# W up and W down in ten pieces with a count for each step, contexts a batch earlier: a fused attention and FP4 feed-forward kernel

## The chip, the cores and the metric

The kernel runs on one NeuronCore of a Trainium2 chip. The metric is the device time of one execution in microseconds (us), from the program's start to its end. The profile gives a span, from the first instruction to the last, which is 1.8 us shorter than the time of the same execution.

## The reference

What is computed, for 16 batches of 256 rows by 256 columns:

```python
# x, ctx: (16, 256, 256); w_gate, w_up: (704, 256); w_down: (256, 704); all float32
q, k, v = heads(layernorm(x)), heads(ctx), heads(ctx)     # 16 heads of 16 columns
x = x + softmax(q @ k.T / 4) @ v                          # for each head
z = layernorm(x)
h = silu(fp4(z) @ fp4(w_gate).T) * (fp4(z) @ fp4(w_up).T)
out = x + fp4(h) @ fp4(w_down).T
# fp4(a): blocks of 16 along the last axis; scale = max(|block|) / 6;
#         each element goes to the nearest of 0, .5, 1, 1.5, 2, 3, 4, 6, times sign and scale
```

## The kernel before, in words

The kernel has two stages: attention over 16 batches (up to about 245 us of the span), then the feed-forward net over 32 tiles of 128 rows (from about 285 us). The change touches the first alone. Each engine has its own hand-written program, and semaphores tie them.

**Attention.** One step of TensorE computes the 16 heads of a batch t: the scores (SC), which ScalarE turns into exponentials (P), and the products with the values (PV). Heads stand as (g, j), four groups of four. In the same step TensorE also computes a second product of queries and keys (MX), 22 heads ahead, for which VectorE finds each row's maximum (`maximum`, MF<-MX). MX has two banks, so that the product of one head waits until the reduction of the head two before it is done (`max_scores`). The maxima of a batch are split into two bfloat16 parts (MP), turned by TensorE, copied by ScalarE (MT), and put by a small DMA (QS<-MT) as two more rows below that batch's queries. The first scores of a batch wait for that DMA (`scores`, semaphore m_stacked).

**SyncE's queue.** Nearly every DMA is issued by SyncE, in order (`attention_step` of SyncE). Its step t waits for the last part of the keys of batch t+3 (k_low) and issues six copies KS<-KP of 128 KB; waits for the maxima of batch t+1 and issues QS<-MT; waits for the third part of the queries of batch t+3 (q_out), which ScalarE writes at the very end of its step t, and issues six copies QS<-QP; then it loads from HBM, 256 KB each, the two layouts QN and KT of batch t+5, the context C of batch t+2, and x (X) of batch t. Since it waits for the end of ScalarE's step t, the second half of SyncE's step t is issued while TensorE is already in step t+1.

**Weights.** The three weight matrices lie in one tile W of 4608 columns, cut into 16 slices of 288. In step t VectorE reduces slice t+1 to its block maxima (`weight_maxima`, wmax<-W), after the reduction of head (1, 1), and later finds scales; GpSimd and ScalarE scale and round; each slice goes through in one step and part of the next. W gate fills the first third of the slices, W up the second, W down the last. W gate is loaded in the first steps; W up and W down are loaded by `load_weights` at the ends of SyncE's steps 0 to 3. VectorE waits for W gate in step 0 and for W up in step 4 (`st.first == RING`), and for W down at the end of step 4.

**Values.** GpSimd copies the context C into the layout of the values (VA<-C), for batch t+1 in step t.

The steps of SyncE from -1 to 14 are made by `steps(sp, attention_step, -1, RING, 1, RING, B - 1, B)`: steps -1 to 3 written out, 4 to 7 in a loop of one turn, the rest written out. The other engines loop over four steps, three times.

Of the kernel before, what the change touches and what calls it, by code (L numbers as in the profile page):

```python
# [12 lines left out]
B, S, D = 16, 256, 256  # L13
H, DK = 16, 16
QT = S // 128
FI = 704
# [18 lines left out]
RING = 4  # L35
IDENTS, CONSTS = 4, 9
AHEAD = 22
LEAD = 3
# [34 lines left out]
def steps(eng, body, begin, start, turns, period, end, count):  # L73


    for t in range(begin, start):
        body(Step(t, count, period))
    with eng.Fori(0, turns) as i:
        for c in range(period):
            body(Step(start + c, count, period, i))  # L80
    for t in range(start + turns * period, end):
        body(Step(t, count, period))
# [6 lines left out]
def ffn_steps(eng, body):  # L89
    steps(eng, body, 0, 5, (TILES - 10) // 2, 2, TILES + 3, TILES)  # L90


def program(nc, x, x_p, ctx_in, ctx_t, wg_in, wu_in, wd_in, out):
# [8 lines left out]
    with es:  # L102
# [6 lines left out]
        def sem(name):  # L109
            return es.enter_context(nc.semaphore(name))  # L110
# [3 lines left out]
        WN = [W[:, m * NT * D:(m + 1) * NT * D].rearrange("p (r c) -> p r c", c=D) for m in range(2)]  # L114
        WD = W[:, 2 * NT * D:].rearrange("p (r c) -> p r c", r=2)
# [96 lines left out]
        sc_ready, exp_done = sem("sc_ready"), sem("exp_done")  # L212
        pv_done, pv_out = sem("pv_done"), sem("pv_out")
        o_den, o_norm, x1_ready = sem("o_den"), sem("o_norm"), sem("x1_ready")
        w_zeroed, w_begun, w_loaded = sem("w_zeroed"), sem("w_begun"), [sem(f"w_loaded{m}") for m in range(3)]
        w_seq, w_scaled, w_abs, w_c, w_grid, w_done = (sem(n) for n in
            ("w_seq", "w_scaled", "w_abs", "w_c", "w_grid", "w_done"))
        ones_ready, ones_last = sem("ones_ready"), sem("ones_last")
# [18 lines left out]
        def tiles(b):  # L237

            return bass.ds(b * (QT * D), QT * D)

        def gate(eng):

            eng.sem_inc(passed, 1)
# [38 lines left out]
        @block.sync  # L282
        def _(sp):
            def load_first(b, r):
                sp.dma_start(QN[r][:, :, :, :, :].rearrange("p q e d a -> p q (e d a)"),
                             xp_d[:, bass.ds(b * QT, QT), :]).then_inc(qn_loaded[r], 16)
                sp.dma_start(KT[r][:, :], t_d[:, bass.ds(b, 1), :].rearrange("p a c -> p (a c)")).then_inc(kt_loaded[r], 16)

            def load_context(b, r):
                sp.dma_start(C[r][:, :, :], c_d[:, bass.ds(b * QT, QT), :]).then_inc(c_loaded[r], 16)  # L290

            def load_x(b, r):
                sp.dma_start(X1[:, tiles(b)].rearrange("p (q c) -> p q c", q=QT),
                             x_d[:, bass.ds(b * QT, QT), :]).then_inc(x_loaded[r], 16)

            def stack(dst, parts, order, r):


                for j, p in enumerate(order):
                    sp.dma_start(dst[j:PROD:6, :, :].rearrange("d h t -> d (h t)"),  # L300
                                 parts[:, p, :]).then_inc(stacked[r], 16)

            def load_blocks(m, w, lo, hi, done):
                sp.dma_start(WN[m][:, lo:hi, :], w[lo * 128:hi * 128, :].rearrange("(r p) c -> p r c", p=128)
                             ).then_inc(done, 16)

            def load_last(m, w):
                full = FI // 128
                sp.dma_start(WN[m][0:FI - full * 128, full, :], w[full * 128:FI, :]).then_inc(w_loaded[m], 16)

            def load_down(r):
                sp.dma_start(WD[:, r, 0:FI], wd_in[128 * r:128 * (r + 1), :]).then_inc(w_loaded[2], 16)

            def load_weights(t):

                if t == -1:
                    load_blocks(0, wg_in, 2, 5, w_loaded[0])
                    load_last(0, wg_in)
                if t == 0:
                    load_blocks(1, wu_in, 0, 3, w_loaded[1])  # L320
                if t == 1:
                    load_blocks(1, wu_in, 3, 5, w_loaded[1])
                    load_last(1, wu_in)
                if t in (2, 3):
                    load_down(t - 2)

            def part(dst, parts, p, rows, r):
                for j in rows:
                    sp.dma_start(dst[j:PROD:6, :, :].rearrange("d h t -> d (h t)"), parts[:, p, :]).then_inc(stacked[r], 16)

            def first_keys(b):

                for n, rows in enumerate(((0, 3, 5), (1, 4))):
                    sp.wait_ge(k_out, 2 * b + n + 1)
                    part(KS[b], KP[b], n, rows, b)
                sp.wait_ge(k_low, b + 1)
                part(KS[b], KP[b], 2, (2,), b)

            def first_queries(b):
                for n, rows in enumerate(((0, 1, 2), (3, 4), (5,))):  # L340
                    sp.wait_ge(q_out, 3 * b + n + 1)
                    part(QS[b], QP[b], n, rows, b)

            load_first(0, 0)
            load_first(1, 1)
            load_first(2, 2)
            first_keys(0)
            first_queries(0)
            first_keys(1)
            first_queries(1)  # L350
            load_context(0, 0)
            sp.wait_ge(w_zeroed, 4)
            load_blocks(0, wg_in, 0, 2, w_begun)
            load_first(3, 3)

            def attention_step(st):
                if st.has(LEAD):
                    r = st.slot(LEAD, RING)
                    sp.wait_ge(k_low, st.times(LEAD, 1, 1))
                    gate(sp)  # L360
                    sp.wait_ge(sc_ready, st.times(0, H, 1))
                    gate(sp)
                    stack(KS[r], KP[st.slot(LEAD, 2)], (0, 1, 2, 0, 1, 0), r)
                if st.has(1):
                    sp.wait_ge(mt_ready, st.times(1, 1, 1))
                    gate(sp)
                    r = st.slot(1, 2)
                    sp.dma_start(QS[st.slot(1, RING)][PROD:ROWS, :, :].rearrange("d h t -> d (h t)"),
                                 MT[r][:, :]).then_inc(m_stacked[r], 16)
                if st.first == -1:  # L370
                    load_context(1, 1)
                    load_weights(-1)
                if st.has(LEAD):
                    sp.wait_ge(q_out, st.times(LEAD, 3, 3))
                    gate(sp)
                    stack(QS[r_q(st)], QP[st.slot(LEAD, 2)], (0, 0, 0, 1, 1, 2), r_q(st))
                if st.has(LOADS):
                    load_first(st.item(LOADS), st.slot(LOADS, RING))
                if st.first >= 0 and st.has(2):
                    load_context(st.item(2), st.slot(2, RING))  # L380
                if st.has(0):
                    load_x(st.item(0), st.slot(0, RING))
                if st.first >= 0:
                    load_weights(st.first)

            def r_q(st):
                return st.slot(LEAD, RING)

            def ffn_step(st):
                if st.has(-3):  # L390
                    r = st.slot(-3, 2)
                    sp.wait_ge(out_ready, st.times(-3, 1, 1))
                    gate(sp)
                    sp.dma_start(o_d[:, bass.ds(st.item(-3), 1), :].rearrange("p a c -> p (a c)"),
                                 OB[r][:, :]).then_inc(stored[r], 16)

            steps(sp, attention_step, -1, RING, 1, RING, B - 1, B)
            attention_step(Step(B - 1, B, RING))
            attention_step(Step(B, B, RING))
            ffn_steps(sp, ffn_step)  # L400
            for r in range(2):
                sp.wait_ge(stored[r], 16 * (TILES // 2))
# [369 lines left out]
        def _(dve):  # L772
# [64 lines left out]
            def weight_maxima(st):  # L837

                if st.first == -SCALE:
                    dve.wait_ge(w_begun, 16)  # L840
                elif st.first == 0:
                    dve.wait_ge(w_loaded[0], 32)
                elif st.first == RING:
                    dve.wait_ge(w_loaded[1], 48)
                dve.wait_ge(w_scaled, st.times(SCALE, 1))
                nc.vector.tensor_reduce(wmax[:, :], blocks(wslice(st, SCALE)), AX.X, ALU.max,
                                        apply_absolute_value=True).then_inc(w_seq, 1)
# [30 lines left out]
            def attention_step(st):  # L878
# [3 lines left out]
                for g in range(NG):  # L882
                    for j in range(HG):
# [18 lines left out]
                            weight_inverses(st)  # L902
                        if (g, j) == (2, 3) and st.has(GRID):
                            round_weights(st)
                        if (g, j) == (3, 3) and st.first == RING:
                            dve.wait_ge(w_loaded[2], 32)
                        if st.first == B - 1 and HG * g + j < LOTS:
                            weights_out(HG * g + j)

# [424 lines left out]
```

## Time and profile before

| | |
|---|---|
| median of 3 runs | 531.11 us (529.82 to 535.19) |
| profiled execution | 529.71 us, span 527.9 us |
| busy in the span | TensorE 486.9 us (92%), VectorE 435.1 (82%), ScalarE 373.8 (71%), GpSimd 302.3 (57%) |
| granted clock | 1.0 all through attention, 0.7 to 0.9 for some 50 us around the change of stages |
| DMA | 48.97 MB, nearly all of it before 245 us, at some 180 to 220 GB/s |
| W up | one load of 384 KB, one of 256 KB, one of 64 KB |
| W down | two loads of 352 KB |

PE is TensorE, PEld its weight loads, DVE VectorE, ACT ScalarE, POOL GpSimd and SP SyncE. A q behind an engine's name is its sequencer: SyncE's DMA issues are shown as SPq, and their duration is the time for which the queue is held, not that of the transfer. L846 is line 846 of the kernel. In a timeline a row can hold several instructions (x6), its second column then reaches from the first one's start to the last one's end, and in brackets stands how long the engine was idle and what ended that.

### The profile page before, as it was taken

What the parts mean: (1) busy time and instruction counts of PE and PEld (TensorE: products, weight loads), DVE (VectorE), ACT (ScalarE), POOL (GpSimd) and SP (SyncE); (2) the same over time, 40 slices, a digit from 0 to 9 for tenths busy, and PEclk for the clock granted to TensorE, in tenths of its full rate; (3) what the DMA queues carried; (4) which work ended last, traced back from release to release, by engine and by line L of the source; (5) the groups of instructions that cost most, each with busy time, mean ns of one, the idle gap of its engine ahead of it and who ended that gap; (6) DMA issues with size and microseconds to landing.
All of it is one profiled execution on the core that took longest, in us unless ns stands there. A gap on an engine that the chain in (4) does not pass through costs nothing.

```text
span 527.9 us, 13628 instructions
## 1 busy us (share of the span) xinstructions
PE 486.9 (92%) x4036; PEld 383.1 (73%) x4036; DVE 435.1 (82%) x1129; ACT 373.8 (71%) x740; POOL 302.3 (57%) x423
## 2 busy tenths in 40 slices
PE   1889899999999999997857899999999999999996
PEld 0245565666666666654437899999999999999996
DVE  3788899899999999886345888898889998889764
ACT  5569899999999999977653565556656566665653
POOL 7754465556566665443144566666676666766542
PEclk9999999999999999999877899999999999999999
DMA  7784878766666666521000000000000000000000
GB/s 215 215 220 126 212 197 220 226 192 178 191 185 182 176 186 179 149 88 43 0 2 0 2 21 20 10 20 20 20 20 10 20 20 20 20 10 21 23 21 30
DMA packets 49985, 48.97 MB, mean 93 GB/s; under 512 B 4768, under 2 KB 47648, under 8 KB 49952
## 3 DMA queue, kind: packets, MB, share of 16 engines
q1 hardware_dynamic: 49952, 48.58, 32.8%
q8 instruction: 15, 0.25, 0.2%
q14 instruction: 18, 0.15, 0.1%
HBM read 18.94 MB, written 4.19 MB: 44 GB/s over the span
## 4 chain that ended last, share of the span: by engine, by line
PE 73%; DVE 7%; issue 5%; POOL 4%; SPq 4%; ACT 4%; DMA 3%; POOLq 0%; DVEq 0%; ACTq 0%
PE SC L1182 22%; PE PV L1182 12%; PE PV L1130 9%; PE MX L1112 9%; PE SC L1098 7%; DVE MF L783 4%; PE T L1207 4%; SPq L300 3%; DMA QS<-MT 2%; PE T L1212 2%; PE T L1077 2%; PE T L1045 2%; PE SC L1207 1%; PE T L1052 1%; ACT P L611 1%
## 5 line engine op out<-in xcount | busy, mean ns | idle before, releaser
L783 DVE TENSOR_REDUCE MF<-MX 128x2 f32<-128x512 f32 x256 | 164.2, 685 | 19.0 <-PE MX L1112 16.2
L611 ACT ACTIVATE P<-SC 128x512 f32<-128x512 f32 x256 | 140.3, 594 | 19.8 <-PE SC L1098 17.8
L1112 PE MATMUL MX<-KS,QS 96*128 96x256 bf16 x512 | 102.9, 284 | 4.3 <-DVE MF L783 2.5
L1098 PE MATMUL SC<-QS,KS 98*128 98x256 bf16 x512 | 98.5, 274 | 3.6 <-DMA QS<-MT 3.5
L534 POOL TENSOR_TENSOR HQ<-HN,hscale 128x704 f32<-128x704 f32 x31 | 43.1, 1391 | 61.3 <-DVE HN L936 61.3
L716 ACT ACTIVATE HH<-T 128x768 fp32r<-128x768 f32 x31 | 25.2, 813 | 67.9 <-PE T L1207 67.9
L1130 PE MATMUL PV<-P,VA 128*32 128x256 f32 x1024 | 70.0, 392 | 0.9 <-ACT OT L620 0.9
L1098 PEld LDWEIGHTS SC<-QS,KS 98*128 98x128 bf16 x512 | 43.4, 97 | 35.7 <-ACT P L611 20.0
L1182 PE MATMUL SC<-WH,XH 128*128 128x352 f32 x256 | 68.7, 350 | 0.0
L1112 PEld LDWEIGHTS MX<-KS,QS 96*128 96x128 bf16 x512 | 43.9, 99 | 31.6 <-DVE MF L783 23.3
L1182 PE MATMUL SC<-WH,XL 128*128 128x352 f32 x256 | 62.9, 327 | 0.0
L1182 PE MATMUL SC<-WL,XH 128*128 128x352 f32 x256 | 62.9, 327 | 0.0
L1130 PEld LDWEIGHTS PV<-P,VA 128*32 128x32 f32 x1024 | 27.3, 110 | 25.6 <-ACT P L611 7.1
L1182 PEld LDWEIGHTS SC<-WL,XH 128*128 128x128 f32 x256 | 45.6, 192 | 0.0
L1182 PEld LDWEIGHTS SC<-WH,XL 128*128 128x128 f32 x256 | 45.3, 191 | 0.1
L521 POOL TENSOR_TENSOR HN<-HN,hinv 128x704 f32<-128x704 f32 x31 | 43.1, 1390 | 1.0 <-DVE hinv L1026 0.9
L916 DVE TENSOR_TENSOR HN<-SC,SG 128x352 f32<-128x352 f32 x64 | 33.3, 521 | 11.3 <-PE SC L1182 10.1
L1182 PEld LDWEIGHTS SC<-WH,XH 128*128 128x128 f32 x256 | 41.4, 194 | 1.6
L685 ACT ACTIVATE SG<-SC 128x352 f32<-128x352 f32 x64 | 29.4, 460 | 18.0 <-PE SC L1182 13.4
L529 POOL TENSOR_TENSOR frstd<-fve,mhalf 128x2 f32<-128x2 f32 x32 | 22.1, 691 | 22.5 <-DVE fve L983 22.5
L486 POOL TENSOR_TENSOR W<-W,WC 128x288 f32<-128x288 f32 (+1 forms) x16 | 12.7, 796 | 38.8 <-DVE WC L857 38.8
L576 ACT ACTIVATE QP<-T 128x512 bf16<-128x512 f32 x48 | 28.6, 595 | 6.5 <-PE T L1052 3.6
(138 smaller groups left out, 1029.8 us busy)
## 6 DMA issues: line engine op xcount, KB each, us to landing
KS<-KP SPq DMA_DIRECT2D x96, 128.0 KB, 3.1
QS<-QP SPq DMA_DIRECT2D x96, 128.0 KB, 2.4
QN<-in_x_p SPq DMA_DIRECT2D x16, 256.0 KB, 3.1
KT<-in_ctx_t SPq DMA_DIRECT2D x16, 256.0 KB, 3.1
C<-in_ctx SPq DMA_DIRECT2D x16, 256.0 KB, 4.2
X<-in_x SPq DMA_DIRECT2D x16, 256.0 KB, 4.9
out<-OB SPq DMA_DIRECT2D x32, 128.0 KB, 1.7
W<-in_L_ffn_w_down SPq DMA_DIRECT2D x2, 352.0 KB, 6.0
```

The lines of the kernel that those rows point to most:

```text
L521: nc.gpsimd.tensor_tensor(blocks(HN[r][:, :]), blocks(HN[r][:, :]), each(hinv[r][:, :]), ALU.mult).then_inc(hm_ready, 1)
L534: nc.gpsimd.tensor_tensor(blocks(HQ[r][:, 0:FI]), blocks(HN[r][:, :]), each(hscale[r][:, :]), ALU.mult).then_inc(hq_ready, 1)
L576: nc.scalar.activation(parts[:, n, :], bank, ACT.Copy).then_inc(out_sem, 1)
L611: nc.scalar.activation(P[g % 2][:, j, :, :], SC[h % 3][:, :, :], ACT.Exp, scale=0.25).then_inc(exp_done, 1)
L685: nc.scalar.activation(SG[a][:, :], G, ACT.Silu).then_inc(silu_done, 1)
L783: nc.vector.tensor_reduce(MF[st.slot(off, 2)][:, :, h:h + 1], MX[h % 2][:, :, :], AX.X, ALU.max, negate=True).then_inc(mx_done, 1)
L916: nc.vector.tensor_tensor(HN[st.slot(0, 2)][:, a * FH:(a + 1) * FH], U, SG[a][:, :], ALU.mult).then_inc(h_done, 1)
L1098: last = nc.tensor.matmul(SC[h % 3][:, k, :], KS[r][0:ROWS, h, k * 128:(k + 1) * 128], QS[r][0:ROWS, h, :], start=True, stop=True)
L1112: last = nc.tensor.matmul(MX[h % 2][:, q, :], QS[r][0:PROD, h, q * 128:(q + 1) * 128], KS[r][0:PROD, h, :], start=True, stop=True)
L1130: last = nc.tensor.matmul(PV[32 * j:32 * (j + 1), g % 2, :], VA[r][:, k, HG * g + j, :], P[g % 2][:, j, k, :], start=(k == 0), stop=(k == ...
L1182: mm = nc.tensor.matmul(dst, x[:, c, :], w[:, c, :], start=(first and i == 0), stop=(last and i == len(chunks) - 1))
L1207: return nc.tensor.matmul(dst, src, ident[:, :], start=first, stop=False, is_transpose=True, skip_group_check=True)
```

## The change

W up and W down are loaded in ten pieces: the five blocks of 128 rows of W up (128 KB each) in SyncE's steps 1 to 5, its last 64 rows (64 KB) in step 6, and each half of W down in two parts of 384 and 320 columns (192 and 160 KB) in steps 7, 8, 10 and 11. A piece stands behind the load of X, the last DMA of its step. Step t signals on one of three semaphores in turn (w_piece). At the end of each step t from 0 to 14, SyncE waits for the piece of step t-1, if there is one, and adds one to w_ready. VectorE waits for the count t ahead of `weight_maxima` in each step t from 1 on, in place of its waits for W up and W down in step 4.

The context is loaded three batches ahead in place of two, ahead of QN and KT in place of behind them. SyncE's steps are all written out.

```diff
-        w_zeroed, w_begun, w_loaded = sem("w_zeroed"), sem("w_begun"), [sem(f"w_loaded{m}") for m in range(3)]
+        w_zeroed, w_begun, w_loaded, w_ready = sem("w_zeroed"), sem("w_begun"), sem("w_loaded"), sem("w_ready")
+        w_piece = [sem(f"w_piece{r}") for r in range(3)]
...
-            def load_last(m, w):
+            def load_last(m, w, done):
                 full = FI // 128
-                sp.dma_start(WN[m][0:FI - full * 128, full, :], w[full * 128:FI, :]).then_inc(w_loaded[m], 16)
-
-            def load_down(r):
-                sp.dma_start(WD[:, r, 0:FI], wd_in[128 * r:128 * (r + 1), :]).then_inc(w_loaded[2], 16)
-
-            def load_weights(t):
-
-                if t == -1:
-                    load_blocks(0, wg_in, 2, 5, w_loaded[0])
-                    load_last(0, wg_in)
-                if t == 0:
-                    load_blocks(1, wu_in, 0, 3, w_loaded[1])
-                if t == 1:
-                    load_blocks(1, wu_in, 3, 5, w_loaded[1])
-                    load_last(1, wu_in)
-                if t in (2, 3):
-                    load_down(t - 2)
+                sp.dma_start(WN[m][0:FI - full * 128, full, :], w[full * 128:FI, :]).then_inc(done, 16)
+
+            def load_down(r, lo, hi, done):
+                sp.dma_start(WD[:, r, lo:hi], wd_in[128 * r:128 * (r + 1), lo:hi]).then_inc(done, 16)
+
+            PIECES = {t + 1: t for t in range(FI // 128 + 1)}
+            DOWN = {7: (0, 0, 384), 8: (0, 384, FI), 10: (1, 0, 384), 11: (1, 384, FI)}
+
+            def load_piece(t):
+
+                done = w_piece[t % 3]
+                if t in DOWN:
+                    load_down(*DOWN[t], done)
+                elif t in PIECES and PIECES[t] < FI // 128:
+                    load_blocks(1, wu_in, PIECES[t], PIECES[t] + 1, done)
+                elif t in PIECES:
+                    load_last(1, wu_in, done)
+
+            def piece_landed(t):
+
+                turns = sum(1 for u in (*PIECES, *DOWN) if u <= t - 2 and u % 3 == (t - 2) % 3)
+                if turns:
+                    sp.wait_ge(w_piece[(t - 2) % 3], 16 * turns)
+                sp.sem_inc(w_ready, 1)
...
                 if st.first == -1:
                     load_context(1, 1)
-                    load_weights(-1)
+                    load_blocks(0, wg_in, 2, 5, w_loaded)
+                    load_last(0, wg_in, w_loaded)
...
+                if st.has(LEAD):
+                    load_context(st.item(LEAD), st.slot(LEAD, RING))
                 if st.has(LOADS):
                     load_first(st.item(LOADS), st.slot(LOADS, RING))
-                if st.first >= 0 and st.has(2):
-                    load_context(st.item(2), st.slot(2, RING))
                 if st.has(0):
                     load_x(st.item(0), st.slot(0, RING))
-                if st.first >= 0:
-                    load_weights(st.first)
+                load_piece(st.first)
+                if 1 <= st.first + 1 < B:
+                    piece_landed(st.first + 1)
...
-            steps(sp, attention_step, -1, RING, 1, RING, B - 1, B)
-            attention_step(Step(B - 1, B, RING))
-            attention_step(Step(B, B, RING))
+            for t in range(-1, B + 1):
+                attention_step(Step(t, B, RING))
...
                 if st.first == -SCALE:
                     dve.wait_ge(w_begun, 16)
                 elif st.first == 0:
-                    dve.wait_ge(w_loaded[0], 32)
-                elif st.first == RING:
-                    dve.wait_ge(w_loaded[1], 48)
+                    dve.wait_ge(w_loaded, 32)
+                else:
+                    dve.wait_ge(w_ready, st.times(0, 1))
...
-                        if (g, j) == (3, 3) and st.first == RING:
-                            dve.wait_ge(w_loaded[2], 32)
```

SyncE, its step 1 from the copies of the queries on and the first copies of step 2; before:

```order
L300 DMA QS<-QP 16x8x512 [waits q_out]
L300 DMA QS<-QP 16x8x512 x5
L285 DMA QN<-in_x_p 128x2x256
L287 DMA KT<-in_ctx_t 128x512
L290 DMA C<-in_ctx 128x2x256
L293 DMA X<-in_x 128x2x256
L304 DMA W<-in_L_ffn_w_up 128x2x256
L309 DMA W<-in_L_ffn_w_up 64x256
L300 DMA KS<-KP 16x8x512 [waits k_low,sc_ready]
```

The same place in the changed kernel, here step 2, which has the first wait for a piece behind it:

```order
L301 DMA QS<-QP 16x8x512 [waits q_out]
L301 DMA QS<-QP 16x8x512 x5
L291 DMA C<-in_ctx 128x2x256
L286 DMA QN<-in_x_p 128x2x256
L288 DMA KT<-in_ctx_t 128x512
L294 DMA X<-in_x 128x2x256
L305 DMA W<-in_L_ffn_w_up 128x256
L301 DMA KS<-KP 16x8x512 [waits w_piece1,k_low,sc_ready]
```

The load of W is one block, C stands first, and ahead of the next keys stands the wait for the piece of the step before, followed by the addition to w_ready, which has no row.

VectorE, inside its loop, around the block maxima of a slice; before:

```order
L782 REGISTER_ALU
L783 TENSOR_REDUCE MF<-MX 128x2 [waits mx_ready]
L845 ISA
L846 ISA [waits w_scaled]
L846 TENSOR_REDUCE wmax<-W 128x18
L782 REGISTER_ALU
L783 TENSOR_REDUCE MF<-MX 128x2 [waits mx_ready]
```

And in the changed kernel:

```order
L791 REGISTER_ALU
L792 TENSOR_REDUCE MF<-MX 128x2 [waits mx_ready]
L853 ISA
L854 REGISTER_ALU [waits w_ready]
L855 ISA [waits w_scaled]
L855 TENSOR_REDUCE wmax<-W 128x18
L791 REGISTER_ALU
L792 TENSOR_REDUCE MF<-MX 128x2 [waits mx_ready]
```

A wait for w_ready now stands between the reductions of heads (1, 1) and (1, 2), in every turn of the loop and in steps 13 and 14 behind it. No other engine's instructions are moved.

## Rows read from the trace of the kernel before

**Rows 1.** Cores: span and mean granted TensorE clock

```profile
core 0: 527.9 us, clock 0.981
```

**Rows 2.** Stretches: us, busy of PE, PEld, DVE, ACT, POOL; clock, DMA share, GB/s

```profile
62.00:76.00 14.00, 12.73 (x128) 8.35 (x128) 11.73 (x30) 11.98 (x25) 7.12 (x12) 1.00 0.81 210
90.00:104.00 14.00, 12.93 (x137) 7.74 (x135) 12.24 (x30) 12.26 (x26) 7.71 (x12) 1.00 0.71 207
...
132.00:146.00 14.00, 13.87 (x146) 8.82 (x145) 13.12 (x32) 13.26 (x29) 8.34 (x13) 1.00 0.68 193
...
244.00:258.00 14.00, 10.28 (x93) 6.20 (x92) 5.88 (x20) 9.21 (x21) 6.00 (x11) 0.88 0.15 40
```

**Rows 3.** Waits: who waited for whom, us in total, times, longest

```profile
POOL VA L471 <- DMA C<-in_ctx: 30.4, 12, 5.6
...
PE SC L1098 <- DMA QS<-MT: 3.5, 5, 1.5
```

**Rows 4.** Timeline of PE at the starts of batches 1 and 2 (start, us)

```profile
47.34 0.28 PE L1098 MATMUL SC<-QS,KS 98*128 98x256 bf16 x1 [0.66 <-DMA QS<-MT]
...
60.57 1.07 PE L1130 MATMUL PV<-P,VA 128*32 128x256 f32 x16
63.14 0.39 PE L1098 MATMUL SC<-QS,KS 98*128 98x256 bf16 x2 [1.50 <-DMA QS<-MT]
```

**Rows 5.** Chain of waits ahead of batch 2 (start, us)

```profile
58.79 4.23 DMA QS<-MT
```

**Rows 6.** DMA issues of W up: KB each, us to landing

```profile
W<-in_L_ffn_w_up SPq DMA_DIRECT2D x1, 384.0 KB, 7.6
```

**Rows 7.** Timeline of ACT: last query part of step 5

```profile
120.51 0.59 ACT L576 ACTIVATE QP<-T 128x512 bf16<-128x512 f32 x1
```

**Rows 8.** Timeline of SyncE's queue, ends of steps 0, 1, 5, 11 and 12

```profile
52.32 0.47 SPq L287 DMA_DIRECT2D KT<-in_ctx_t  x1
53.23 0.37 SPq L290 DMA_DIRECT2D C<-in_ctx  x1
53.65 0.46 SPq L293 DMA_DIRECT2D X<-in_x  x1
54.16 0.46 SPq L304 DMA_DIRECT2D W<-in_L_ffn_w_up  x1
...
68.05 0.47 SPq L293 DMA_DIRECT2D X<-in_x  x1
...
121.19 3.80 SPq L300 DMA_DIRECT2D QS<-QP  x6
125.03 0.60 SPq L285 DMA_DIRECT2D QN<-in_x_p  x1
...
126.70 0.47 SPq L293 DMA_DIRECT2D X<-in_x  x1
...
209.89 0.51 SPq L293 DMA_DIRECT2D X<-in_x  x1
...
224.16 0.49 SPq L293 DMA_DIRECT2D X<-in_x  x1
```

**Rows 9.** Timeline of DVE around wmax in steps 1, 2, 6, 12 and 13

```profile
52.75 0.44 DVE L846 TENSOR_REDUCE wmax<-W 128x18 f32 x1
...
68.56 0.44 DVE L846 TENSOR_REDUCE wmax<-W 128x18 f32 x1
...
126.37 0.44 DVE L846 TENSOR_REDUCE wmax<-W 128x18 f32 x1
...
126.92 1.29 DVE L783 TENSOR_REDUCE MF<-MX 128x2 f32<-128x512 f32 x2
...
210.58 0.44 DVE L846 TENSOR_REDUCE wmax<-W 128x18 f32 x1
...
224.41 0.44 DVE L846 TENSOR_REDUCE wmax<-W 128x18 f32<-128x288 f32 x1
```

**Rows 10.** Timeline of PE: max-product of head (2, 1), step 6

```profile
128.27 0.39 PE L1112 MATMUL MX<-KS,QS 96*128 96x256 bf16 x2
```

## The prediction

> **What bounds it now.** I read the span and clock first [rows 1], then the busy time by stretch [rows 2], then who waits for whom [rows 3], and last the queues of one attention step side by side [rows 4 to 10]. The profiled execution takes 529.7 us against a median of 531.1 us of the three runs shown, so it lies 1.4 us under the median; the sum below is made against the 529.7. In an undisturbed stretch of attention TensorE is busy 13.87 of 14.00 us and VectorE 13.12 [rows 2], and one batch takes 14.03 us. So TensorE sets the pace and VectorE has under one microsecond to spare. The three stretches 62:76, 90:104 and 244:258 show TensorE under that: the first two hold waits for the small transfer of the maxima (QS<-MT), of which there are five with 3.5 us together and 1.5 us at most [rows 3]. 0.66 us of it lies before batch 1 and 1.50 us before batch 2 [rows 4]; the other three, before batches 3, 4 and 5, share 3.5 - 0.66 - 1.50 = 1.3 us. That of batch 2 is seen in the chain of waits: the transfer takes 4.23 us [rows 5], behind the 384 KB of W up issued at 54.16, which took 7.6 us to land [rows 6, 8].
>
> **How one step runs.** I call the start of batch t's scores on TensorE the start of step t. Take t = 6. ScalarE ends the last query part of the step before at 120.51 + 0.59 = 121.10 [rows 7]. Only then can SyncE issue the six QS<-QP copies, and behind them the loads: the last one, X, ends its issue at 126.70 + 0.47 = 127.17 [rows 8]. All this belongs to SyncE's step 5, so SyncE is well into the time of step 6 when its step 5 ends. VectorE reads the slice's maxima (wmax) of step 6 at 126.37 [rows 9], which is 0.80 us before that.
>
> **The change part by part.**
>
> *A new wait on VectorE.* SyncE now adds one to w_ready at the end of each step 0 to 14, and VectorE waits ahead of wmax in step t for the count t, thus for the end of SyncE's step t-1. Before, only steps -1, 0 and 4 waited for weights. This is the term that decides. For t = 6: SyncE is through X 0.80 us after VectorE wants to go on; the piece of W issued behind X costs what the W load cost, 0.51 us from one start to the next (53.65 to 54.16) [rows 8]; and wait, count, and VectorE's two waits take time that no row has by itself. Its bounds are 0.06 us (a max-product follows the reduction that frees its bank by about that, 128.21 to 128.27) [rows 9, 10] and 0.4 us (the gap between KT's end and C's start at 52.79 to 53.23, a SyncE gap with nothing to issue) [rows 8]; nothing of it can be below zero, since it stands between two things in order. I take 0.20, nearer the lower end, as four short sequencer steps. So VectorE stands still 0.80 + 0.51 + 0.20 = 1.51 us.
>
> Does that reach TensorE? Queued behind wmax on VectorE are the reductions of the next heads. They start 0.55 us after wmax and take 1.29 us for two, thus end at 128.21 [rows 9]; the max-product that needs the second one's bank starts at 128.27 [rows 10], 0.06 us later, as tight as two engines get. So there is no slack, and TensorE, which runs in order, loses all of the wait. Nothing gives it back: TensorE has 0.13 us idle in a step.
>
> The same for the other steps. Eight steps (3 to 9 and 11) are like t = 6: 8 x 1.51 = 12.08 us. Step 1: X ends at 53.65 + 0.46 = 54.11, wmax at 52.75 [rows 8, 9], no piece yet: 1.36 + 0.20 = 1.56. Step 2: X ends at 68.52, wmax at 68.56 [rows 8, 9], but wmax stands there 1.50 us late because of the wait before batch 2, which goes (below): 1.46 + 0.51 + 0.20 = 2.17. Step 10 has no piece ahead: 1.00. Step 12, where the layouts are loaded no more: X ends 210.40, wmax 210.58, with a piece: -0.18 + 0.71 = 0.53. Step 13, without: 224.65 against 224.41, 0.24 + 0.20 = 0.44 [rows 8, 9]. Step 14 waits for nothing. Sum 12.08 + 1.56 + 2.17 + 1.00 + 0.53 + 0.44 = 17.8 us more.
>
> *The big W loads gone from steps 0 to 3.* No W stands ahead of the KS<-KP copies of step 1, and 128 KB instead of 320 to 352 in the next three. The transfer of the maxima is ready as late as TensorE lets it, while the KS<-KP copies ahead of it hang on statistics made before wmax. With VectorE's stall in between, the queue has 1.5 us more to drain. So all four waits from batch 2 on go: 3.5 - 0.66 = 2.9 us less. That of batch 1 stays. What is late next is VectorE, priced above.
>
> *Pieces in steps 1 to 8, 10 and 11.* Ten issues in place of five (two up, one last rows, two down). Their data, at most 192 KB, goes beside the step, with a whole step until it is asked for. Their issues lie on the path, since VectorE waits for the count behind them; they are in the 17.8. Cost as transfers: nothing, covered by the 1.5 us just named. If that cover were gone, the maxima's transfer would be late by up to 1.5 us as before batch 2.
>
> *Contexts a batch earlier and ahead of the layouts.* GpSimd waits 30.4 us in 12 waits for them [rows 3]. It hides: TensorE and VectorE show no wait on it (VA is wanted a batch later). The same four loads in another order end at the same time; the extra context goes to step -1, when SyncE afterwards waits for GpSimd anyway. Zero. *The loop of SyncE written out* had one turn of four steps: the same instructions, zero.
>
> Sum: 17.8 - 2.9 = 14.9 us, thus 529.7 + 14.9 = 544.6 us.
>
> *A rule against pieces.* SyncE's issue of W took 0.46 us [rows 8] and it went on at once, so a piece costs the queue 0.51 us. The Trainium skill (DMA: Bandwidth & Descriptors, section Rules for kernel authors) says to coalesce many small transfers, and its section on the anatomy of one DMA gives some 2.0 us fixed for each on the GpSimd path. Were the queue held so long for each of ten pieces, the page's estimate would be 10 x 1.5 = 15 us more, near 560 us. The same section lays most of it to completion, not to the issue, and by that the trace agrees.
>
> **Rivals.**
>
> (a) *The count comes in time, or VectorE's stall is hidden.* Then only the 2.9 us count: 526.8 us, no slower than before. The mechanism is the empty queue; it decides if SyncE ends its step 1.5 us sooner against VectorE than I read, at 126.37 instead of 127.88. For it: nothing in the rows of steps 3 to 11; steps 12 and 13 come near. Against it: six copies of 3.80 us cannot start before ScalarE's 121.10. That the change does not do what it says, with the wait satisfied early, is this case too. Chance 0.07.
>
> (b) *Part of the stall is absorbed.* VectorE has 14.00 - 13.12 = 0.88 us idle in a step. If half of it lay behind wmax, 13 x 0.44 = 5.7 us come back: 538.9 us. Against it, 128.21 and 128.27. Chance 0.12.
>
> (c) *TensorE's clock falls in the new pauses.* Between 244 and 258 us TensorE was busy 10.28 of 14 us and granted 0.88 of the clock [rows 2], a mix of 2.4 and 1.2 GHz: 12% of 14 us is 1.7 us. In thirteen steps that is 22 us: 567 us. Against it: busy 12.73 and 12.93 of 14 us, with the 1.5 us pause among them, kept 1.00 [rows 2], and 13.87 of 15.5 is the like of it. By the Trainium skill (TensorE: Matmul & The Clock Gate, section HAM oscillation) a waiting pause in every round can throttle the array each round; no run here shows it in attention. Chance 0.05.
>
> My forecast has 0.76.
>
> **Numbers.** The likeliest time is 544.6; measured beside a median like the one shown it would read some 0.5 us more, 545. The forecast alone, with 0.06 and 0.4 for the signal (13 x -0.14 and 13 x +0.2) and 1.4 us for the median, runs from 542 to 549. The range takes in (b) below and a little above: 538 to 550. About 1% (5.3 us) is what a measurement of this kernel can tell from no change. Forecast, (b) and (c) are slower by over 1%; of (a) most is within 1% (526.8 is 0.6% less). Faster 0.02, same 0.06, slower 0.92.
>
> **What would show it.** VectorE idle before each wmax of steps 1 to 13 by 1.0 to 2.2 us, in steps 12 and 13 by half of one; the batches of steps 3 to 9 15.5 us apart instead of 14.03; max-products waiting for MF in (2,0) and (2,1); no wait of TensorE for QS<-MT but that of batch 1; GpSimd's 30 us wait for contexts gone, with nothing gained by it; clock 1.00 until 250 us. I am wrong if wmax has no idle time ahead of it, or if it has and the batches stay 14 us apart.

## The result

| | before | changed |
|---|---|---|
| median of the runs of one session | 531.85 us (529.82 to 535.19, 4 runs) | 543.33 us (542.41 to 545.56, 4 runs) |
| ratio | | 1.0216 (95% interval 1.0153 to 1.0278) |
| profiled execution, its span | 529.71, 527.9 us | 543.28, 541.5 us |
| a second session | 531.68 us (19 runs) | 543.70 us (4 runs), ratio 1.0208 (1.0160 to 1.0256) |

The change makes the kernel 2% slower. Forecast were 545 us (538 to 550), and 544.6 against the profiled execution, which measured 543.3.

### The profile page after: what moved, and what is told of

The parts are those of the page before. It is cut to its first block, busy times and chain, and to the rows that moved or that the text cites. A ratio compares the mean times of both kernels' runs of the same rounds, so it can differ in the third digit from the quotient of the medians.

```text
span 541.5 us, 13656 instructions
## 1 busy us (share of the span) xinstructions
PE 493.0 (91%) x4036; PEld 384.1 (71%) x4036; DVE 434.1 (80%) x1129; ACT 375.2 (69%) x740; POOL 301.9 (56%) x423
## 4 chain that ended last, share of the span: by engine, by line
PE 60%; SPq 13%; issue 8%; ACT 7%; DVE 6%; POOL 3%; DMA 1%; DVEq 0%; ACTq 0%; POOLq 0%
PE SC L1189 21%; PE PV L1189 12%; SPq L301 7%; PE MX L1119 6%; PE PV L1137 5%; PE SC L1105 4%; ACT P L620 4%; PE T L1214 4%; DVE MF L792 3%; PE T L1219 2%; PE T L1052 2%; ACT QP L585 1%; PE SC L1214 1%; SPq L291 1%; SPq L286 1%
## 5 line engine op out<-in xcount | busy, mean ns | idle before, releaser
L792 DVE TENSOR_REDUCE MF<-MX 128x2 f32<-128x512 f32 x256 | 163.1, 685 | 16.0 <-PE MX L1119 14.9
L1105 PE MATMUL SC<-QS,KS 98*128 98x256 bf16 x512 | 99.9, 278 | 0.7 <-DMA QS<-MT 0.7
```

The lines of the kernel that those rows point to most:

```text
L792: nc.vector.tensor_reduce(MF[st.slot(off, 2)][:, :, h:h + 1], MX[h % 2][:, :, :], AX.X, ALU.max, negate=True).then_inc(mx_done, 1)
L1105: last = nc.tensor.matmul(SC[h % 3][:, k, :], KS[r][0:ROWS, h, k * 128:(k + 1) * 128], QS[r][0:ROWS, h, :], start=True, stop=True)
```

## The profile after

The list of waits of the changed kernel (engine, line, waited for: us in total, times, longest) has a new row high up, with the sequencer of SyncE as the releaser:

```profile
POOL W L495 <- DVE WC L866: 86.7, 16, 10.9
...
DVE wmax L855 <- SPq L333: 17.7, 13, 2.2
...
PE MX L1119 <- DVE MF L792: 14.1, 19, 1.8
```

VectorE waits 17.7 us in 13 steps for the count; the forecast had 17.8 us in 13. TensorE in its turn waits for VectorE's reductions. GpSimd's wait for contexts [rows 3] is not in the list any more, but GpSimd has won nothing: it now stands longer in its next wait, for WC. The waits for the maxima's transfer, 3.5 us of TensorE in [rows 3], are nearly gone. The page's costliest groups show it in the scores' row (last columns: busy, mean ns; idle before, releaser):

```profile
L1105 PE MATMUL SC<-QS,KS 98*128 98x256 bf16 x512 | 99.9, 278 | 0.7 <-DMA QS<-MT 0.7
```

One step in full, the same batch 6 as in [rows 7 to 10], which now starts at 127.22. First ScalarE's last query part, then SyncE's queue:

```profile
126.77 0.59 ACT L585 ACTIVATE QP<-T 128x512 bf16<-128x512 f32 x1
```

```profile
127.45 3.79 SPq L301 DMA_DIRECT2D QS<-QP  x6
131.29 0.59 SPq L291 DMA_DIRECT2D C<-in_ctx  x1
131.92 0.50 SPq L286 DMA_DIRECT2D QN<-in_x_p  x1
132.47 0.47 SPq L288 DMA_DIRECT2D KT<-in_ctx_t  x1
132.98 0.44 SPq L294 DMA_DIRECT2D X<-in_x  x1
133.46 0.47 SPq L305 DMA_DIRECT2D W<-in_L_ffn_w_up  x1
134.57 1.86 SPq L301 DMA_DIRECT2D KS<-KP  x3
```

The piece's issue ends at 133.93. VectorE has been through its reductions since 131.42 + 1.29 = 132.71 and goes on at 134.15:

```profile
131.42 1.29 DVE L792 TENSOR_REDUCE MF<-MX 128x2 f32<-128x512 f32 x2
134.15 0.45 DVE L855 TENSOR_REDUCE wmax<-W 128x18 f32 x1 [1.44 <-SPq L333]
134.52 2.47 DVE L792 TENSOR_REDUCE MF<-MX 128x2 f32<-128x512 f32 x4
```

From the end of the issue to wmax it is 0.22 us, where I had taken 0.20. TensorE stands still two heads later, and only there:

```profile
133.86 0.38 PE L1105 MATMUL SC<-QS,KS 98*128 98x256 bf16 x2
135.26 0.39 PE L1119 MATMUL MX<-KS,QS 96*128 96x256 bf16 x2 [1.02 <-DVE MF L792]
135.49 0.38 PE L1105 MATMUL SC<-QS,KS 98*128 98x256 bf16 x2
135.85 0.39 PE L1119 MATMUL MX<-KS,QS 96*128 96x256 bf16 x2
```

The product at 135.26 is that of head (2, 0); it waits for the first reduction behind wmax. That of (2, 1), at 135.85, follows 0.59 us later, at VectorE's pace, where it was 0.45 us before (127.82 to 128.27). The stretches of the batches from 2 on, us, busy of PE, PEld, DVE, ACT, POOL, clock, DMA share, GB/s, show what became of a step [rows 2]:

```profile
64.20:80.34 16.14, 14.20 (x148) 8.77 (x145) 13.17 (x32) 13.43 (x28) 8.35 (x13) 1.00 0.68 174
80.34:95.67 15.33, 14.21 (x149) 8.77 (x145) 13.17 (x32) 13.38 (x28) 8.58 (x15) 1.00 0.65 182
95.67:111.80 16.13, 14.20 (x149) 8.76 (x145) 13.16 (x32) 13.38 (x28) 8.48 (x15) 1.00 0.65 174
...
127.22:142.65 15.43, 14.28 (x148) 8.76 (x144) 13.26 (x32) 13.48 (x28) 8.46 (x14) 1.00 0.68 180
```

Steps 1 to 7 take 15.3 to 15.4 us, but 16.1 in steps 2 and 4, where a single issue of SyncE lasted 1.41 and 1.25 us. No engine is full any more: the step runs from SyncE's loads to VectorE to TensorE and round again. In the chain of waits over 126.88 to 135.26 (start, us) one reads it whole, eleven DMA issues in a row where before no issue of SyncE stood on the path of a steady step:

```profile
126.88 0.49 ACT QP L585
127.40 0.05 issue
127.45 0.56 SPq L301
...
133.46 0.47 SPq L305
133.93 0.05 issue
134.03 0.06 DVEq L855
134.09 0.05 issue
134.15 0.06 DVE wmax L855
...
134.52 0.69 DVE MF L792
135.21 0.05 issue
135.26 0.39 PE MX L1119 x2
```

## The experiments

All times are medians, and ratios are to the kernel before in the same session, with the 95% interval. Theory A is that of the prediction: the whole loss is VectorE's wait for a count that stands behind the loads in SyncE's queue. Its rivals: B, the ten smaller transfers or the contexts' new place cost the time; F, a count in each step costs by itself.

**The count ahead of the query copies** (e1). In the changed kernel:

```diff
+                if 1 <= st.first + 1 < B:
+                    piece_landed(st.first + 1)
                 if st.has(LEAD):
                     sp.wait_ge(q_out, st.times(LEAD, 3, 3))
...
                 load_piece(st.first)
-                if 1 <= st.first + 1 < B:
-                    piece_landed(st.first + 1)
```

Expected: 

> The changed kernel, but SyncE adds to w_ready ahead of its wait for the last query part, in place of behind the loads; pieces and contexts are as in the change. Theory A (VectorE's wait for a count that stands behind the loads is the whole loss): the count of a step comes some 9 us sooner, VectorE's 17.7 us wait for it is gone, and the loads of W gone from the first steps are left as a gain: 526.8 us, at most 529. Theory B (the ten small transfers or the new place of the contexts cost the time): it stays at 540 us or more.

Measured: 530.2 us, ratio 0.9987 (0.9954 to 1.0020). No wait for the count is left, and with it the whole loss is gone; pieces and contexts are still there. B falls. But the time is that of before, not 526.8 us: the gain that I had given to the W loads gone from steps 0 to 3 is missing. The waits show where it went:

```profile
PE SC L1105 <- DMA QS<-MT: 3.5, 4, 1.1
```

TensorE waits as long for the maxima's transfer as before, in other steps: before batches 2, 4, 6 and 10. In this profile TensorE also ran at the lower of its two clock levels until 40.4 us, where it reached the higher one before 32 us in the kernel before. A pair of matmuls took 0.63 us there and 0.38 later, and step 0 was 1.1 us longer than before; this may be why there is no wait before batch 1:

```profile
37.27 0.63 PE L1119 MATMUL MX<-KS,QS 96*128 96x256 bf16 x2
...
40.44 0.38 PE L1105 MATMUL SC<-QS,KS 98*128 98x256 bf16 x2
```

The last wait, before batch 10, is behind a piece of W down (160 KB) issued 5.2 us ahead of the transfer. That the piece makes it late is not shown: the larger piece of the step before (192 KB) was followed by no such wait. In this order on TensorE:

```profile
176.64 1.07 PE L1137 MATMUL PV<-P,VA 128*32 128x256 f32 x16
178.75 0.39 PE L1105 MATMUL SC<-QS,KS 98*128 98x256 bf16 x2 [1.03 <-DMA QS<-MT]
```

**Nothing but the count, in the kernel before** (e2).

```diff
                 if st.first >= 0:
                     load_weights(st.first)
+                if 1 <= st.first + 1 < B:
+                    sp.sem_inc(w_ready, 1)
...
-                elif st.first == RING:
-                    dve.wait_ge(w_loaded[1], 48)
+                if st.first >= 1:
+                    dve.wait_ge(w_ready, st.times(0, 1))
+                if st.first == RING:
+                    dve.wait_ge(w_loaded[1], 48)
```

Expected: 

> The kernel before, with nothing but the count: SyncE adds one to w_ready at the end of each step 0 to 14, VectorE waits for it ahead of the block maxima in each step from 1 on; loads of W and contexts are as before. Theory A: VectorE waits 2.1 us in step 1, 2.7 in step 2, 1.4 in steps 3 and 4, 1.0 in steps 5 to 11, 0.4 in step 13, together 15 us; some 2 us of it is absorbed, and 2.9 us of waits for the maxima's transfer go: 529.7 + 10 = 540 us. Theory B: no more than 531 us.

Measured: 544.7 us, ratio 1.0245 (1.0167 to 1.0323). The wait alone makes the loss, without pieces and contexts; VectorE stands still 15.8 us, 15 were expected:

```profile
DVE wmax L851 <- SPq L387: 15.8, 12, 2.9
```

All the large loads of W stand where they stood, and yet TensorE has only the wait before batch 1 left for the maxima's transfer, 0.6 us of 3.5: VectorE's stall takes the others away by itself. The run is 4 to 5 us slower than theory A had it. Two of its steps are longer than their stall explains, and the clock says why (section on what was not expected).

**The contexts alone, in the kernel before** (e3).

```diff
+                if st.has(LEAD):
+                    load_context(st.item(LEAD), st.slot(LEAD, RING))
                 if st.has(LOADS):
                     load_first(st.item(LOADS), st.slot(LOADS, RING))
-                if st.first >= 0 and st.has(2):
-                    load_context(st.item(2), st.slot(2, RING))
```

Expected: 

> The kernel before, with nothing but the contexts loaded three batches ahead and in front of the layouts. Theory A: GpSimd's 30 us of waits for contexts go and nothing else moves: within 1 us of before, 529 to 531 us. Theory C (contexts ahead of the layouts make the layouts late, and with them statistics and keys): slower by 2 us or more, with VectorE's statistics waiting for QN.

Measured: 531.3 us, ratio 1.0019 (0.9982 to 1.0056): no difference that can be told. GpSimd's waits for contexts are gone, its wait for WC grew from 38.8 to 71.3 us.

**The count between X and the piece** (e4).

```diff
-                load_piece(st.first)
                 if 1 <= st.first + 1 < B:
                     piece_landed(st.first + 1)
+                load_piece(st.first)
```

Expected: 

> The changed kernel, but the count is added between X and the piece. Theory A: the ten steps whose count stood behind a piece's issue (2 to 9, 11 and 12) win 0.51 us each: 543.3 - 5.1 = 538.2 us, VectorE's wait for the count 12.6 us in place of 17.7. Theory B: no change, 543 us.

Measured: 536.6 us, ratio 1.0107 (1.0036 to 1.0177). VectorE waits 10.2 us in place of 17.7:

```profile
DVE wmax L855 <- SPq L333: 10.2, 12, 1.5
```

That is 7.5 us less, where 5.1 were expected: from step 6 on, the steps with a piece lose the 0.5 us of its issue (0.3 to 0.6), and the surplus lies in steps 1, 2, 4, 5 and 13. In all but step 5 SyncE's single long issues fell otherwise in the two executions; ahead of step 5 TensorE itself had waited 0.59 us for the maxima's transfer in e4. The medians of the two sessions differ by 6.8 us. The loss follows the place of the count; by B nothing should have moved.

**VectorE's maxima later in the step** (g3), the changed kernel with SyncE as it is:

```diff
-                        if (g, j) == ((1, 1) if st.first > 0 else (3, 3)) and st.has(SCALE):
+                        if (g, j) == ((2, 0) if st.first > 0 else (3, 3)) and st.has(SCALE):
                             weight_maxima(st)
```

Expected: 

> The changed kernel with one edit: VectorE's block maxima of the slice stand behind the reduction of head (2, 0) in place of (1, 1), 1.9 us later in the step, SyncE's order is untouched. Theory A: the count (6.9 us into the step, 7.7 in steps 2 and 4) is there when VectorE comes (7.9 us), the 17.7 us wait falls under 1 us, and the time is that of the run with the count early, 530 us. Theory F (a count for each step costs by itself, by the instructions and the signal): it stays at 540 us or more.

Measured: 531.4 us, ratio 0.9997 (0.9969 to 1.0025). The count, its instructions and its place are unchanged, and VectorE does not wait for it any more, since it comes later: 7.88 us into the step (127.44 - 119.56), where it was 5.41 before. F falls. In VectorE's timeline wmax has no idle time ahead of it:

```profile
125.51 2.01 DVE L792 TENSOR_REDUCE MF<-MX 128x2 f32<-128x512 f32 x3 [0.47 <-PE MX L1119]
127.44 0.44 DVE L855 TENSOR_REDUCE wmax<-W 128x18 f32 x1
127.80 0.68 DVE L792 TENSOR_REDUCE MF<-MX 128x2 f32<-128x512 f32 x1
```

The later place of wmax is not quite free: steps 6 to 10 take 14.14 to 14.31 us, where the kernel before has 14.01 to 14.10 and e1, with the same count, 14.05 to 14.14 in steps 6 to 8. That is some 0.2 us a step. The equal time hides it: TensorE's waits for the maxima's transfer are 2.2 us here for 3.5 before, and from batch 15 to the end this profile is 2.2 us shorter.

**The changed kernel again**, in that session.

Expected: 

> The changed kernel unchanged, on the same chip as the three others, for its ratio to the kernel before: 1.022 as in the first runs, 1.015 to 1.028.

Measured: 543.7 us, ratio 1.0208 (1.0160 to 1.0256). VectorE's wait is 17.7 us again.

**Context and piece in SyncE's idle time** (g1). The run with the count early left the waits for the maxima's transfer open: does the load queue make them, or SyncE's long issues?

```diff
                 if 1 <= st.first + 1 < B:
                     piece_landed(st.first + 1)
+                if st.has(LEAD):
+                    load_context(st.item(LEAD), st.slot(LEAD, RING))
+                load_piece(st.first)
                 if st.has(LEAD):
                     sp.wait_ge(q_out, st.times(LEAD, 3, 3))
...
-                if st.has(LEAD):
-                    load_context(st.item(LEAD), st.slot(LEAD, RING))
...
-                load_piece(st.first)
-                if 1 <= st.first + 1 < B:
-                    piece_landed(st.first + 1)
```

Expected: 

> As the run with the count early, but context and piece of W are issued right behind the maxima's transfer, in SyncE's idle time ahead of the last query part, and no longer behind the query copies. Theory D (the maxima's transfer is late because loads crowd the queue ahead of the key copies): the four waits of TensorE for it, 3.5 us, fall under 1 us, and the time is 3 us under the run with the count early: 527 us. Theory E (they come from SyncE's single long issues of 1.3 to 1.6 us, whatever is queued): the waits stay at 3 us or more, 530 us.

Measured: 527.5 us, ratio 0.9915 (0.9879 to 0.9951); run again in another session, 527.1 us, 0.9908 (0.9870 to 0.9946). This is the first version that beats the kernel before. Batches 6 to 12 start 14.01 to 14.02 us apart. Late are batches 1, 4 and 5, which start 0.64, 0.68 and 0.46 us after the product ahead of them; before batches 4 and 5 a key copy's issue of 1.57 and 1.39 us stands ahead of the transfer. So both theories hold a part: of the 3.5 us in e1, 2.4 went with the loads out of the way, and 1.1 us before batches 4 and 5 stay, behind the long issues.

**X in the gap too** (g2), `load_x` moved to the same place.

Expected: 

> As g1, and X is issued in the same gap, so that only the two layouts stand between the query copies and the next key copies. Theory D: no wait for the maxima's transfer but perhaps that of batch 1, 526.5 us. A rival: with C, X and a piece in the gap (up to 704 KB) the query copies behind them land late and the max-products wait for them: 530 us or more.

Measured: 527.6 us, ratio 0.9922 (0.9889 to 0.9955). No more than g1, and no loss: neither the gain of half a microsecond nor the rival came.

**The large loads in the gap** (h1), the kernel before without count and pieces:

```diff
                 if st.first == -1:
                     load_context(1, 1)
                     load_weights(-1)
+                if st.first >= 0 and st.has(2):
+                    load_context(st.item(2), st.slot(2, RING))
+                if st.first >= 0:
+                    load_weights(st.first)
                 if st.has(LEAD):
                     sp.wait_ge(q_out, st.times(LEAD, 3, 3))
...
-                if st.first >= 0 and st.has(2):
-                    load_context(st.item(2), st.slot(2, RING))
...
-                if st.first >= 0:
-                    load_weights(st.first)
```

Expected: 

> The kernel before with its few large loads of W and contexts two batches ahead, but both issued behind the maxima's transfer, in SyncE's idle time; no count, no pieces. Theory G (only the place in the queue counts, size and number of the W loads do not): as fast as g1, 527.5 us, 0.8% under before. Theory H (pieces are what keeps the queue short): W up's 384 KB and W down's 352 KB hold up the query copies behind them or the next maxima's transfer, 530 us or more.

 And for g1 beside it: 

> The kernel g1 unchanged, beside h1 on the same chip: 0.992 of before, as in its first runs. Theory G: h1 within 0.5% of it. Theory H: h1 slower by 0.5% or more.

Measured: h1 526.7 us, ratio 0.9890 (0.9849 to 0.9932); g1 beside it 527.1 us, 0.9908. The pieces bring nothing; the place in the queue brings the whole 0.8 to 1.1%. In SyncE's queue one sees why it is free, the load of 384 KB standing in a pause of the queue:

```profile
45.39 0.68 SPq L368 DMA_DIRECT2D QS<-MT  x1
46.12 0.41 SPq L290 DMA_DIRECT2D C<-in_ctx  x1
46.57 0.47 SPq L304 DMA_DIRECT2D W<-in_L_ffn_w_up  x1
48.01 3.78 SPq L300 DMA_DIRECT2D QS<-QP  x6
```

## Why the prediction was right

*The wait and its size.* Right: 17.7 us in 13 steps for 17.8, 1.44 us of idle time in step 6 for 1.51, 0.22 us for the signal where I took 0.20, and with no wait in step 14. That the sum is so near is partly luck, since single steps missed both ways: step 4 stood still 2.23 us for 1.51, because the issue of X took 1.25 us, and step 9 1.24 us for 1.51. The 2.17 us of step 2 (2.24 measured) had a long issue of the trace before in them without my seeing it (the six query copies from 61.68 took 4.66 us in place of 3.80), and one fell in the same place again. Moving the count (e1), moving VectorE's place (g3), adding the count alone (e2) and shortening what stands ahead of it (e4) each moved the time as the wait did. This is shown, not argued.

*All of it reaches TensorE.* Nearly. The step went from 14.04 to 15.43 us, by 1.39, while wmax came 1.52 us later in its step (134.15 - 127.22 = 6.93 against 126.37 - 120.96 = 5.41). The slack that I called none was none: the product of head (2, 1) starts 8.63 us into the step for 7.31 before, 1.32 later. What I passed over lies ahead of it, on VectorE itself: the reduction behind wmax follows it by 0.37 us (134.15 to 134.52) where it was 0.55 [rows 9], and this goes with the stall: it is 0.37 in each of the 13 steps with a wait and 0.55 to 0.57 in steps 1 to 12 of e1, which has the same instructions and no wait. Why is open; g3 has 0.36 at another place with no stall at all. That is 0.18 us a step, some 2.2 us in all: rival (b) in kind, with 0.4 of its size.

*The W loads gone from steps 0 to 3 are worth 2.9 us.* The sum came out, its first reason did not. In the changed kernel the waits did go (0.7 us left), but through the second reason that I gave, VectorE's stall: the key copies are issued ahead of it and have 1.4 us more to land. With the stall and all large loads (e2) the waits are gone as well, but for batch 1; where the stall is taken away (e1) they are back at 3.5 us, though no large load is left. So the price that I put on rival (a), 526.8 us, was wrong by 3.4 us, and beside the kernel before of its own session e1 won nothing of the 2.9. I had put the wait before batch 2 down to the 384 KB alone. In e1 it is 1.07 us with no W ahead of it, for 1.50 before, and in both a single long issue of QN (1.49 and 1.44 us) stands ahead of the key copies.

*The pieces cost nothing as transfers, the contexts nothing.* The first holds as long as VectorE's stall is their cover, as the prediction said. Without it e1 has 1.0 us before batch 10 behind a piece, but no run shows that the piece is the cause. The contexts: shown, by e3. The 2.0 us fixed for a transfer that the Trainium skill gives for the GpSimd path (DMA: Bandwidth & Descriptors, section on the anatomy of one DMA) do not stand in SyncE's queue here: by e4 a piece costs it about its issue, 0.3 to 0.6 us a step.

*The sum.* From the start of batch 0 to that of batch 15 it is 213.9 us before and 226.6 us in the changed kernel, 12.7 more: 17.7 of stall, less 2.8 of other waits, less 2.2 absorbed. The start of batch 0 is 1.4 us later in this execution (33.60 against 32.19) and the end 0.5 us nearer. The first is chance: the same kernel started batch 0 at 32.28 in its second profile. Forecast were 14.9, measured 13.6. So the forecast was too high by the 2.2 us absorbed, and the 1.4 us of chance bring the profiled time nearer to it than the mechanism does. From median to median the change costs 11.5 us (543.33 - 531.85).

*Rival (c), the clock.* Given 0.05 and not seen in the profile after, where the clock is 1.00 in all steps shown. It did come in other executions, in one or two steps of each; see below. With a cost of 1.4 to 1.5 us a step, it is a small part of what I had priced, for all 13.

## What to carry to other kernels

A semaphore count is as late as the place in the queue where it is added: a wait that replaces one long satisfied must be put beside the time at which the queue reaches that place, not beside the landing of the data. When two engines hand work to and fro with 0.06 us between them, as here, a wait of either goes to the bound nearly whole. Moving the wait behind three more reductions took it away and cost some 0.2 us a step in its place. Before splitting transfers, look for a pause in the queue that issues them: here their place was worth 1%, their size nothing.

## What was not expected of the hardware

**The clock fell after pauses of 1.6 to 2.9 us inside busy attention.** Three executions show it. The changed kernel's second profile, steps 0 to 3:

```profile
32.28:47.35 15.07, 13.73 (x120) 7.35 (x120) 13.66 (x32) 13.53 (x27) 7.20 (x11) 1.00 0.61 178
47.35:64.88 17.53, 15.62 (x144) 9.21 (x145) 13.21 (x33) 13.24 (x27) 7.18 (x12) 0.90 0.60 152
64.88:82.62 17.74, 15.55 (x147) 9.64 (x145) 13.40 (x32) 13.42 (x28) 8.36 (x13) 0.90 0.61 158
82.62:97.94 15.32, 14.05 (x148) 8.78 (x145) 13.16 (x32) 13.39 (x28) 8.59 (x15) 1.00 0.67 182
```

The granted clock of 0.90 is a mix of 2.4 and 1.2 GHz; TensorE's busy time grows by 1.4 to 1.5 us against the steps at 1.00. Ahead of each fall TensorE stood still once, 1.92 us in step 2 and here 1.63 us in step 1:

```profile
56.00 0.39 PE L1119 MATMUL MX<-KS,QS 96*128 96x256 bf16 x2 [1.63 <-DVE MF L792]
```

With the count alone (e2) it was 0.90 and 0.91 in steps 2 and 4, behind pauses of 2.0 and 2.4 us. With the contexts alone (e3) the clock fell within one wait of 2.91 us for the maxima's transfer, which took the next step to 0.82 and 16.27 us, all of it busy:

```profile
64.43:80.70 16.27, 16.27 (x145) 10.02 (x145) 13.22 (x31) 13.34 (x27) 6.34 (x10) 0.82 0.58 167
```

In the first profile of the changed kernel pauses of up to 1.8 us left it at 1.00. So a like pause sometimes costs its own length and sometimes 1.4 us more; what tells the cases apart, these runs do not say. The Trainium skill (TensorE: Matmul & The Clock Gate, section HAM oscillation) tells of a kernel whose waits for DMA, some 3 to 5 us each, throttle the array again. The three executions agree with it in kind; their pauses were shorter.

**A DMA issue that takes 0.8 to 1.9 us in place of 0.4 to 0.7** comes three to six times in each profile of attention, before as after, most of them between 50 and 106 us. The twelve profiles have 56 such issues, and every one of them overlaps in time with a 16 KB packet of the instruction queue; 17 other packets that fall on an issue leave it at its usual length. So the two go together, but what holds the issue was not tested. The long issues delay the key copies, and with them, by the order in SyncE's queue, the starts of batches 4 and 5, in the fastest version too.
